# The ranking of edges by source runs inside the first walk, and part of its stores in the first node stage (graph network kernel, one core)

## The chip, the cores and the metric

The kernel runs on one core of a Trainium2 chip, as one program. The metric is the device time of that program in microseconds; the median of several runs is compared. The engines are TensorE (PE), VectorE (DVE), ScalarE (ACT), GpSimd (POOL) and SyncE (SP). Each has its own in-order queue of instructions and waits on semaphores. SP and ACT start ordinary transfers; indirect ones (gathers and scatters by an index per row) are started by GpSimd.

## The reference

Four layers of graph networks follow each other on 50000 nodes of 128 values and 25000 edges (src, dst), which come sorted by dst. The change touches the sort of the edges by source and the first layer alone:

```python
def _L0_gnn_ref(feat, W_neigh, b_neigh, src, dst):
    msgs = feat[src]
    neigh_sum = jax.ops.segment_sum(msgs, dst, num_segments=N)
    deg = jax.ops.segment_sum(jnp.ones(src.shape[0], feat.dtype), dst, num_segments=N)
    h_neigh = neigh_sum / jnp.maximum(deg, 1.0)[:, None]
    h = jnp.concatenate([feat, h_neigh], axis=1)
    return h @ W_neigh + b_neigh
...
def _gcn2_layer(x, W, beta, row, col, norm, num_nodes):
    h = jax.ops.segment_sum(norm[:, None] * x[col], row, num_segments=num_nodes)
    xp = (1.0 - ALPHA) * h + ALPHA * x
    return (1.0 - beta) * xp + beta * (xp @ W)
```

The result of each layer is added to its input and normalised. The second layer (two rounds of `_gcn2_layer`) sums over the edges of each source, so it needs the edges grouped by source. The layers behind it (two attention layers) use the order by dst.

## The kernel before

Nodes are padded and cut into 98 blocks of 512 rows and 196 tiles of 256 rows; edges into 196 columns of 128 edges (`J`), one edge per partition. The program is a row of phases; each ends with a barrier of all engines.

1. `lay_out_sorted` writes the edges in order of dst to memory and tests that they are sorted; they are, so two further sort passes are skipped.
2. `sort_pass` "s2" orders the edges by the upper digit of their source (196 digit values, 256 nodes each). VectorE makes one-hot rows of each column's digits, 28 groups of 7 columns (line 286), and TensorE sums them to a histogram (line 333). After prefix sums, the one-hots are made again; for each column TensorE adds the four columns before it to a running count (line 354), and VectorE reads each edge's place out of it (line 316, two instructions). VectorE writes the places of each group (line 321) and its payload, two words an edge, and GpSimd scatters them, one indirect store per column (line 365). Beside it, behind the ranks in the queues of TensorE and VectorE, the tables by dst are made: `walk_tables` "d" (lines 798 to 865) and `edge_tables` "e" (lines 471 to 521).
3. `walk_tables` "s" makes the same table by source ("sw_").
4. `walk` "e0" sums neighbours by dst. GpSimd gathers the source rows of the 196 columns (line 906); a table tells TensorE for each of 396 steps which column and which tile meet, each step being 2 products (4 matmuls in the trace, line 948) with one-hots of VectorE (line 921). ScalarE opens and empties the PSUM banks (lines 1018, 1021), SP stores each tile. A counter `ready` tells TensorE which gathers have landed.
5. `node_sage` goes over the 98 blocks in a pipeline of lags. Per block GpSimd does seven small instructions: the counts (`degree`, lines 1339 to 1343), the reciprocal root and shift (`deviation`, lines 1348 to 1352) and a factor (`factor`, line 1358). ScalarE's normalisation waits for the second, its store for the third. VectorE takes means and statistics (line 1451: the neighbour sums times the reciprocal degree), TensorE transposes and multiplies.
6. Two more walks by source, "e1a" and "e1b", and the other layers follow.

In the order listings below, and in the trace, a tile's name has its phase in front (`s_` or `e_`), and `e_bank` is the PSUM of the first walk.

Of the kernel before, what the change touches and what calls it, by code (L numbers as in the profile page):

```python
# [22 lines left out]
F32, I32, F16, BF16, U16 = mybir.dt.float32, mybir.dt.int32, mybir.dt.float16, mybir.dt.bfloat16, mybir.dt.uint16  # L23
ALU, ACT, AX = mybir.AluOpType, mybir.ActivationFunctionType, mybir.AxisListType

P = 128
# [4 lines left out]
SLOT = 6  # L31
NB = -(-NODES // BLOCK)
NPAD = NB * BLOCK
GC, SLOTS = 7, 4
TURN = GC * SLOTS
# [7 lines left out]
WS = 2  # L43
# [175 lines left out]

def sort_pass(nc, keep, name, words, digits, high, load, target, beside=None):  # L220

    with Phase(nc, name, freed="written") as ph:
# [26 lines left out]
        with nc.Block() as block:  # L251
            n_loads = load(block, ph, pay, loaded)
            more = ph.stack.enter_context(ExitStack())

# [104 lines left out]
            def _(pool):  # L359
# [8 lines left out]
                for s in range(SLOTS):  # L368
                    done(pool, scattered, TURNS - 1, s, 16 * GC)

            if beside is not None:
                with nc.allow_non_contiguous_dma(reason="one word of an edge's payload"):
                    beside(block, more, banks, lambda pe: pe.wait_ge(ranked, J + 4))

# [506 lines left out]

def walk(nc, keep, name, e, rows, table, summed, out, start):

# [4 lines left out]
    with Phase(nc, name) as ph:  # L888
# [7 lines left out]
        start.memory(ph)  # L896
        with nc.Block() as block:
            @block.gpsimd
            def _(pool):
                def landed(g):  # L900
                    pool.wait_ge(got[g % 7], 64 * (g // 7 + 1))
                    pool.sem_inc(ready, 1)

                for g in range(J // 4):
                    for c in range(4 * g, 4 * g + 4):
                        pool.indirect_dma_start(out=rows[:, c, 0:fetched], out_offset=None, in_=table,  # L906
                                                in_offset=bass.IndirectOffsetOnAxis(ap=e.other_i[:, c:c + 1], axis=0))\
                            .then_inc(got[g % 7], 16)
                    if g >= 2:
                        landed(g - 2)  # L910
                landed(J // 4 - 2)
                landed(J // 4 - 1)

            @block.vector
# [364 lines left out]

def node_sage(nc, keep, x_turned, agg, w, bias, y1):  # L1280

# [4 lines left out]
    with Phase(nc, "n0", freed="turned added stored y_ready x1_ready sums_ready meaned inverted") as ph:  # L1286
# [19 lines left out]
        sums_ready, rstd_ready, cleared, norm_step = (  # L1306
            slot_sems(ph, "sums_ready"), slot_sems(ph, "rstd_ready"), ph.sem("cleared"), ph.sem("norm_step"))
        with nc.Block() as block:
            @block.sync
# [19 lines left out]
            def _(pool):  # L1329
# [29 lines left out]

                pipeline(pool, (0, degree), (4, deviation), (4, factor))  # L1360

# [1585 lines left out]
def gnn(nc, x, x_turned, src, dst, attr, sage, gcn, gat2, gat, out):  # L2947
# [12 lines left out]
    with ExitStack() as stack:  # L2960
# [10 lines left out]
        with ExitStack() as walk_stack:  # L2971
            on_dst, lay_out_walk = walk_tables(nc, keep, "d", by_dst[1], WD, None, stack, krel_rows)

            def tables_on_dst(block, more, banks, banks_free):
                lay_out_walk(block, more, banks, banks_free)
                lay_out_edges(block, more, banks)

            sort_pass(nc, keep, "s2", WS, HIGH, True, load_edges(nc, src, dst, None), by_src, tables_on_dst)
            on_src = walk_tables(nc, keep, "s", by_src, WS, walk_stack)
            with nc.sbuf_tensor("x_rows", [P, J, ROW], F32) as rows:  # L2980
                walk(nc, keep, "e0", on_dst, rows, x, ROW, agg_dst, FromZero(ROW))
            node_sage(nc, keep, x_turned, agg_dst, sage["W"], sage["b"], y1)
            with nc.sbuf_tensor("y_rows", [P, J, ROW], F32) as rows:
                walk(nc, keep, "e1a", on_src, rows, y1, D, m1, FromRows(y1))
                walk(nc, keep, "e1b", on_src, rows, m1, D, z2, FromScaledRows(m1))
# [49 lines left out]
```

## Time and profile before

| | |
|---|---|
| median of 3 runs | 6525.23 us (6518.1 to 6535.32) |
| the profiled execution: its time | 6517.36 us |
| its span | 6515.6 us |
| TensorE busy | 3738.5 us, 57% |
| VectorE busy | 3242.0 us, 50% |
| ScalarE busy | 2301.1 us, 35% |
| GpSimd busy | 3518.2 us, 54% |
| mean granted clock of TensorE | 0.772 |

Busy shares are averages over stages with different limits, so no row of this table says what bounds one stage. Windows (stretches of the span in us from its start) and the timeline do. An indirect transfer counts on GpSimd as long as GpSimd makes its descriptors; its landing comes later.

### The profile page before, as it was taken

Reading aid. Unit: us, or ns where it says so; the run is one execution under the profiler, and the core shown is the slowest. Engines: PE = TensorE matmul, PEld = TensorE weight load, DVE = VectorE, ACT = ScalarE, POOL = GpSimd, SP = SyncE. Lnnn points to the kernel's source line nnn. Section 1 sums busy time; section 2 is a strip of 40 time slices with the busy share of each in tenths; the row PEclk is TensorE's granted clock in tenths of the full one; section 3 lists DMA queues with packets and bytes.
Section 4 is the critical chain, followed back from the end, with each engine's and each line's share of the span. In section 5 each row is a group of like instructions: output and inputs, shape, how many; then the busy total and the mean of one; then the engine's idle time right before and its main releaser. Section 6 shows DMA issues by size and latency. Waiting matters only on the chain. (4 is left out here: it accounts for less than half of the span.)

```text
span 6515.6 us, 102955 instructions
## 1 busy us (share of the span) xinstructions
PE 3738.5 (57%) x23719; PEld 2732.5 (42%) x23720; DVE 3242.0 (50%) x13277; ACT 2301.1 (35%) x6649; POOL 3518.2 (54%) x4631
## 2 busy tenths in 40 slices
PE   4421579715615685566669769998010089813566
PEld 3320568515615664233322256766010067612466
DVE  5330248503302485344467668886125178722577
ACT  0000347505504574233323258886000044400166
POOL 3647107771271055544406568887735755574398
PEclk7555799858857998888879889999555599955588
DMA  1012239625625796511101034443230189723276
GB/s 35 1 31 58 82 123 281 203 66 159 180 66 150 195 285 202 173 34 33 33 7 33 31 106 141 139 143 126 64 89 30 37 285 293 250 55 82 85 226 203
DMA packets 593072, 784.65 MB, mean 120 GB/s; under 512 B 138946, under 2 KB 362870, under 8 KB 592330
## 3 DMA queue, kind: packets, MB, share of 16 engines
q1 hardware_dynamic: 431734, 533.20, 27.0%
q0 software_dynamic: 62848, 112.43, 7.0%
q10 hardware_dynamic: 98328, 137.22, 5.7%
q8 instruction: 57, 0.93, 0.1%
q14 instruction: 105, 0.86, 0.0%
HBM read 470.23 MB, written 317.95 MB: 121 GB/s over the span
## 5 line engine op out<-in xcount | busy, mean ns | idle before, releaser
L2754 POOL TENSOR_SCALAR n_hot<-node_of,d_krel 128x256 f32<-128x256 f32 x396 | 366.6, 958 | 178.1 <-ACTq L2810 176.8
L1736 PE MATMUL lg_z_ps<-gat_wl,lg_tr 128*128 128x512 f32 x392 | 242.2, 703 | 254.1 <-issue 123.9
L948 PE MATMUL e_bank<-x_rows,e_hot 128*128 x1584 | 224.5, 292 | 273.1 <-issue 219.1
L948 PE MATMUL e1b_bank<-y_rows,e1b_hot 128*128 x1584 | 223.7, 290 | 270.4 <-issue 232.1
L948 PE MATMUL e1a_bank<-y_rows,e1a_hot 128*128 x1584 | 225.3, 291 | 265.3 <-issue 232.6
L1713 POOL DMA_INDIRECT lg_rows<-x,e_other_i x196 | 185.4, 946 | 311.2 <-PE lg_at_ps L1729 240.5
L906 POOL DMA_INDIRECT y_rows<-m,s_other_i x196 | 188.0, 959 | 306.4 <-POOLq L102 246.4
L1233 ACT ACTIVATE n_r<-n_r,n_shift,n_rstd 128x128 f32<-128x128 f32 x784 | 321.7, 480 | 79.0 <-POOL n_shift L1224 73.9
L689 POOL DMA_INDIRECT agg<-e_msg,e_put_i x196 | 193.7, 988 | 256.2 <-DVEq L718 195.8
L1792 DVE TENSOR_TENSOR lg_z<-lg_z_ps,lg_z 128x512 f32<-128x512 f32 x196 | 135.4, 691 | 391.4 <-issue 206.2
L948 PEld LDWEIGHTS e_bank<-x_rows,e_hot 128*128 128x128 f32 x1584 | 203.8, 201 | 294.1 <-issue 294.0
L948 PEld LDWEIGHTS e1b_bank<-y_rows,e1b_hot 128*128 128x128 f32 x1584 | 203.1, 202 | 291.1 <-issue 291.1
L948 PEld LDWEIGHTS e1a_bank<-y_rows,e1a_hot 128*128 128x128 f32 x1584 | 203.8, 203 | 287.1 <-issue 287.1
L2782 PE MATMUL n_bank<-h_rows,n_hot 128*128 x1584 | 248.0, 331 | 131.3 <-ACT n_bank L2816 113.3
L1499 POOL TENSOR_TENSOR n_rstd<-n_mv,minus_half 128x4 f32<-128x4 f32 x98 | 103.7, 1059 | 392.5 <-DVE n_mv L1592 392.5
L620 POOL DMA_INDIRECT agg_dst<-e_rows,e_put_i x196 | 203.3, 1037 | 194.6 <-DVEq L647 135.2
L921 DVE TENSOR_SCALAR e1b_hot<-node_of,s_krel 128x256 f32<-128x256 f32 x396 | 110.8, 350 | 386.1 <-remote 191.7
L921 DVE TENSOR_SCALAR e1a_hot<-node_of,s_krel 128x256 f32<-128x256 f32 x396 | 111.4, 352 | 379.0 <-issue 144.4
L921 DVE TENSOR_SCALAR e_hot<-node_of,d_krel 128x256 f32<-128x256 f32 x396 | 110.8, 350 | 378.5 <-remote 162.1
L2782 PEld LDWEIGHTS n_bank<-h_rows,n_hot 128*128 128x128 f32 x1584 | 240.4, 244 | 139.5 <-issue 139.5
L1233 ACT ACTIVATE n_o<-n_y_ps,n_shift,n_rstd 128x128 f32<-128x128 f32 x784 | 293.6, 458 | 13.0 <-POOL n_shift L1503 12.2
L365 POOL DMA_INDIRECT by_src<-s_pay_s,s_place_i x196 | 188.5, 962 | 171.9 <-DVE s_pay_s L322 112.8
(529 smaller groups left out, 12353.4 us busy)
## 6 DMA issues: line engine op xcount, KB each, us to landing
n_ag<-agg_dst SPq DMA_DIRECT2D x196, 264.0 KB, 3.8
n_hs<-h SPq DMA_DIRECT2D x196, 264.0 KB
n_xs<-x SPq DMA_DIRECT2D x196, 256.0 KB, 4.2
agg_dst<-e_ev SPq DMA_DIRECT2D x196, 132.0 KB
y<-n_o ACTq DMA_DIRECT2D x98, 264.0 KB, 3.5
e1a_fed<-y SPq DMA_DIRECT2D x196, 132.0 KB
m<-e1a_ev SPq DMA_DIRECT2D x196, 132.0 KB
e1b_fed<-m SPq DMA_DIRECT2D x196, 132.0 KB
```

Source lines behind the costliest of these rows:

```text
L365: pool.indirect_dma_start(out=target, out_offset=bass.IndirectOffsetOnAxis(ap=place_i[:, s, k:k + 1], axis=0), in_=pay_s[:, s, k, :], in_o ...
L620: pool.indirect_dma_start(out=agg, out_offset=bass.IndirectOffsetOnAxis(ap=e.put_i[:, c:c + 1], axis=0), in_=rows[:, c, :], in_offset=None ...
L689: pool.indirect_dma_start(out=agg, out_offset=bass.IndirectOffsetOnAxis(ap=e.put_i[:, c:c + 1], axis=0), in_=msg[:, g % SLOTS, k, 0:out_wi ...
L906: pool.indirect_dma_start(out=rows[:, c, 0:fetched], out_offset=None, in_=table, in_offset=bass.IndirectOffsetOnAxis(ap=e.other_i[:, c:c + ...
L921: ins = dve.tensor_scalar(hot[:, s, k, :], keep.node_of[:, :], e.krel[:, bass.ds(turn * (HOTS * STEPB) + s * STEPB + k, 1)], None, ALU.is_ ...
L948: ins = pe.matmul(bank[:, bass.ds(to + h * width, summed)], hot[:, s, k, h * P:(h + 1) * P], flat_rows[:, bass.ds(row, summed)], start=Fal ...
L1233: ins = act.activation(out[:, g, 0:D], r[:, g, :], ACT.Identity, bias=shift[:, g:g + 1], scale=rstd[:, g:g + 1])
L1713: pool.indirect_dma_start(out=rows[:, g % SLOTS, k, i, :], out_offset=None, in_=x, in_offset=bass.IndirectOffsetOnAxis(ap=of[:, c:c + 1], ...
L1736: pe.matmul(z_ps[q][:, :], tr[:, q, 0, :], g.wl[:, :], start=True, stop=False)
L1792: dve.tensor_tensor(z[:, c % 2, :], z_ps[c % 2][:, :], z[:, c % 2, :], ALU.max).then_inc(z_out, 1)
L2754: ins = pool.tensor_scalar(hot[:, i // STEPB % HOTS, i % STEPB, :], keep.node_of[:, :], e.krel[:, i:i + 1], None, ALU.is_equal)
L2782: ins = pe.matmul(bank[:, bass.ds(to + h * 256, SUMMED)], hot[:, s, k, h * P:(h + 1) * P], flat_rows[:, bass.ds(row, SUMMED)], start=False ...
```

## The change

The sort by source is no phase of its own. The tables by dst are made in a phase "t" without it. A class `BySource` makes the ranks at the head of the first walk's instructions on VectorE and TensorE (`rank`), using the walk's PSUM. GpSimd first starts the walk's 196 gathers, then scatters the first `EARLY` = 112 columns (`scatter_early`). The 84 others are scattered in `node_sage`, one per block, by a fourth stage `sort` of GpSimd's pipeline, which is now written out instead of a loop. Places and payload of all columns stay in memory on the chip. The table by source comes after `node_sage`.

```diff
+EARLY = 112
...
+class BySource:
...
+    def rank(self, nc, keep, ph, block, banks):
...
+        @block.scalar
+        def _(act):
+            act.wait_ge(ends_in, 16 * WS)
+            for i in range(WS):
+                act.activation(pay[:, :, i], ends[:, i, :], ACT.Copy).then_inc(loaded, 1)
...
+            with dve.Fori(0, TURNS) as turn:
+                for s in range(SLOTS):
+                    dve.wait_ge(hot_used, turn * SLOTS + s + 1)
+                    hot(turn, s, digs_ready, first_hot)
...
+                    for k in range(GC):
+                        c = s * GC + k
+                        dve.wait_ge(run_ready, turn * TURN + c + 1)
+                        dve.tensor_tensor_reduce(junk[:, c % 4, :], onehot[:, s, k, :], run_ps[c % 4][:, 0:digits],
+                                                 1.0, 0.0, ALU.mult, ALU.add, place[:, s, k:k + 1]).then_inc(ranked, 1)
+                    dve.wait_ge(ranked, turn * TURN + (s + 1) * GC + 4)
+                    dve.tensor_copy(self.place_i[:, bass.ds(turn * TURN + s * GC, GC)], place[:, s, :]).then_inc(self.placed, 1)
...
+            pe.wait_ge(ranked, J + 4)
...
+    def scatter_early(self, pool):
+
+        pool.wait_ge(self.loaded, WS)
+        for c in range(EARLY):
+            pool.wait_ge(self.placed, c // GC + 1)
+            self.scatter(pool, c, self.scattered[c // 4 % 7])
+            if c % 4 == 3 and c >= 11:
+                g = c // 4 - 2
+                pool.wait_ge(self.scattered[g % 7], 64 * (g // 7 + 1))
+        for g in (EARLY // 4 - 2, EARLY // 4 - 1):
+            pool.wait_ge(self.scattered[g % 7], 64 * (g // 7 + 1))
+        pool.wait_ge(self.placed, J // GC)
...
         with nc.Block() as block:
+            if by_source is not None:
+                by_source.rank(nc, keep, ph, block, bank[:, :].rearrange("p (b w) -> p b w", b=RING))
+
...
                 landed(J // 4 - 2)
                 landed(J // 4 - 1)
+                if by_source is not None:
+                    by_source.scatter_early(pool)
...
-                pipeline(pool, (0, degree), (4, deviation), (4, factor))
+                def sort(turn, s):
+
+                    k = turn * SLOT + s
+                    c = k + EARLY
+                    if k >= 8 and c - 8 < J:
+                        pool.wait_ge(sorted_in[k % 8], 16 * (k // 8))
+                    if c < J:
+                        by_source.scatter(pool, c, sorted_in[k % 8])
+
+                pipeline(pool, (0, degree), (4, deviation), (4, factor), (0, sort), written_out=True)
...
-            sort_pass(nc, keep, "s2", WS, HIGH, True, load_edges(nc, src, dst, None), by_src, tables_on_dst)
...
+            with ExitStack() as source_stack:
+                by_source = BySource(nc, source_stack, src, dst, by_src)
+                with nc.sbuf_tensor("x_rows", [P, J, ROW], F32) as rows:
+                    walk(nc, keep, "e0", on_dst, rows, x, ROW, agg_dst, FromZero(ROW), by_source)
+                node_sage(nc, keep, x_turned, agg_dst, sage["W"], sage["b"], y1, by_source)
             on_src = walk_tables(nc, keep, "s", by_src, WS, walk_stack)
-            with nc.sbuf_tensor("x_rows", [P, J, ROW], F32) as rows:
-                walk(nc, keep, "e0", on_dst, rows, x, ROW, agg_dst, FromZero(ROW))
-            node_sage(nc, keep, x_turned, agg_dst, sage["W"], sage["b"], y1)
```

Three places where the order of instructions moves. TensorE at the head of the first walk, before: the banks are opened by 8 matmuls and the loop of the walk begins.

```order
L928 MATMUL e_bank<-iota_h,ident_h 128x264 x8
L932 UNCONDITIONAL_BRANCH
L932 ISA
L937 TENSOR_LOAD d_table
L937 ISA
```

TensorE at the same place of the changed kernel (its own line numbers): histogram loop, sums, then the loop of the ranks (its first rows).

```order
L971 MATMUL e_bank<-iota_h,e_zero_h 128x196
L973 UNCONDITIONAL_BRANCH
L973 ISA
L977 MATMUL e_bank<-e_onehot,ident_h 128x196 x7
...
L980 MATMUL e_bank<-iota_h,e_zero_h 128x196
L983 MATMUL e_bank<-e_hist,ones_h 128x196
L984 MATMUL e_bank<-e_hist,tri_h 128x196
L987 MATMUL e_bank<-e_base,ident 128x196 x4
L989 UNCONDITIONAL_BRANCH
L989 ISA
L996 MATMUL e_bank<-e_onehot,ident_h 128x196 x4
```

The rows of before come after these loops now. GpSimd in the walk and up to the first block of the node stage, changed kernel; before, line 906 (now 1048) was followed by the barrier at once:

```order
L1048 DMA x_rows<-x,d_other_i 128x128 x196
L1004 DMA by_src<-by_src_pay,by_src_place_i 25088x2 x112
L1036 UNCONDITIONAL_BRANCH
L101 ISA
L1473 UNCONDITIONAL_BRANCH
L1484 TENSOR_TENSOR n_q<-n_ag,ones 128x4
L1486 TENSOR_TENSOR n_part<-n_q,n_ninths 128x4
L1488 TENSOR_TENSOR n_part<-n_part,ones 128x4
```

112 stores stand between the last gather and the end of the phase. GpSimd in the loop of the node stage before, from one block's counts to the next one's:

```order
L1339 TENSOR_TENSOR n_q<-n_ag,ones 128x4
L1341 TENSOR_TENSOR n_part<-n_q,n_ninths 128x4
L1169 REGISTER_ALU
L1343 TENSOR_TENSOR n_part<-n_part,ones 128x4
L1348 TENSOR_TENSOR n_rstd<-n_mv,minus_half 128x4
L1169 ISA
L1350 TENSOR_TENSOR n_shift<-n_mv,n_rstd 128x4
L1169 REGISTER_ALU
L1352 TENSOR_TENSOR n_shift<-n_shift,minus_one 128x4
L1358 TENSOR_TENSOR n_o<-n_part,n_q 128x4
```

And in the changed kernel:

```order
L1484 TENSOR_TENSOR n_q<-n_ag,ones 128x4
L1486 TENSOR_TENSOR n_part<-n_q,n_ninths 128x4
L1488 TENSOR_TENSOR n_part<-n_part,ones 128x4
L1493 TENSOR_TENSOR n_rstd<-n_mv,minus_half 128x4
L1495 TENSOR_TENSOR n_shift<-n_mv,n_rstd 128x4
L1497 TENSOR_TENSOR n_shift<-n_shift,minus_one 128x4
L1503 TENSOR_TENSOR n_o<-n_part,n_q 128x4
L1004 DMA by_src<-by_src_pay,by_src_place_i 25088x2
```

The register instructions are gone, and one store stands between a block's factor and the next block's counts.

## Rows read from the trace of the kernel before

**Rows 1.** Windows of scatters, of the walk with gathers and without, of the node stage.
```profile
86.00:258.00 172.00, 73.50 (x440) 55.96 (x440) 66.53 (x372) 0.00 (x0) 107.75 (x112) 0.56 0.02 1
...
455.00:690.00 235.00, 31.59 (x86) 23.44 (x86) 7.13 (x24) 6.76 (x20) 176.98 (x185) 0.51 0.22 57
...
712.00:940.00 228.00, 181.50 (x1445) 169.78 (x1444) 98.20 (x354) 122.61 (x364) 0.00 (x0) 0.98 0.31 109
957.00:1238.00 281.00, 272.72 (x2037) 229.08 (x2038) 232.11 (x1156) 208.08 (x667) 207.17 (x673) 0.99 0.87 274
```

**Rows 2.** Tile x_rows: matmuls and gathers, ns min/median/max, first and last start.
```profile
L948 PE MATMUL e_bank<-x_rows,e_hot x1584: 276/276/585, 447.0 to 938.8; 128*128 x198
L906 POOL DMA_INDIRECT x_rows<-x,d_other_i x196: 940/944/1795, 440.3 to 687.7; - x196
```

**Rows 3.** Timeline of TensorE in the first walk: start us, us, instruction, idle before.
```profile
439.54 1.92 PE L928 MATMUL e_bank<-iota_h,ident_h 128*128 128x264 f16 x8 [4.15 <-PEq L102]
446.98 8.01 PE L948 MATMUL e_bank<-x_rows,e_hot 128*128 x44 [5.52 <-POOLq L902]
...
501.94 0.38 PE L948 MATMUL e_bank<-x_rows,e_hot 128*128 x1 [2.41 <-issue]
...
712.63 0.38 PE L948 MATMUL e_bank<-x_rows,e_hot 128*128 x1 [1.03 <-issue]
714.76 1.23 PE L948 MATMUL e_bank<-x_rows,e_hot 128*128 x4 [1.75 <-issue]
```

**Rows 4.** Windows: attention edges with and without gathers, attention sum, first and later part.
```profile
2800.00:3200.00 400.00, 274.80 (x839) 133.82 (x840) 183.68 (x1024) 127.82 (x419) 194.54 (x205) 0.82 0.13 34
3300.00:3345.00 45.00, 44.69 (x158) 22.40 (x157) 32.42 (x185) 23.51 (x78) 0.00 (x0) 1.00 0.00 0
4935.00:4980.00 45.00, 0.00 (x0) 0.00 (x0) 40.58 (x91) 0.00 (x0) 34.35 (x34) 0.50 0.12 40
4980.00:5080.00 100.00, 0.00 (x0) 0.00 (x0) 33.17 (x76) 0.00 (x0) 77.45 (x75) 0.50 0.12 39
```

**Rows 5.** Timeline of GpSimd and VectorE around the table work.
```profile
32.73 0.36 POOL L394 CAST s_pay<-s_ends 128x196 f32<-128x196 int32 x1 [19.49 <-DMA s_ends<-dst]
...
384.49 0.40 DVE L798 CAST dw_key_i<-dw_pay 98x256 int32<-98x256 f32 x1
...
422.73 0.15 DVE L516 TENSOR_SCALAR e_split<-et_whole 128x1 f32<-128x1 f32 x1
...
438.08 0.57 DVE L836 SCALAR_TENSOR_TENSOR s_krel<-sw_tile_off,sw_banks 128x396 f32<-128x396 f32 x1
```

**Rows 6.** The sort: line 333, then timeline of VectorE and GpSimd.
```profile
L333 PE MATMUL s_banks<-s_onehot,ident_h x196: 245/257/373, 36.4 to 76.5; 128*128 128x196 f16 x196
...
85.23 0.17 DVE L321 CAST s_place_i<-s_place 128x7 int32<-128x7 f32 x1
...
91.45 0.17 DVE L321 CAST s_place_i<-s_place 128x7 int32<-128x7 f32 x1
...
86.44 1.22 POOL L365 DMA_INDIRECT by_src<-s_pay_s,s_place_i  x1 [53.05 <-DVE s_pay_s L322]
...
262.86 1.01 POOL L365 DMA_INDIRECT by_src<-s_pay_s,s_place_i  x1 [4.73 <-DVE s_pay_s L322]
```

**Rows 7.** Timeline of GpSimd and VectorE in the node stage.
```profile
956.82 0.73 POOL L1343 TENSOR_TENSOR n_part<-n_part,ones 128x4 f32<-128x4 f32 x1
...
956.79 0.69 DVE L1451 TENSOR_TENSOR n_ag<-n_ag,n_rq 128x512 f32<-128x512 f32 x1
...
1100.56 1.01 POOL L1348 TENSOR_TENSOR n_rstd<-n_mv,minus_half 128x4 f32<-128x4 f32 x1 [0.39 <-DVE n_mv L1440]
...
1102.77 0.20 POOL L1343 TENSOR_TENSOR n_part<-n_part,ones 128x4 f32<-128x4 f32 x1
1103.40 1.01 POOL L1348 TENSOR_TENSOR n_rstd<-n_mv,minus_half 128x4 f32<-128x4 f32 x1 [0.43 <-DVE n_mv L1440]
```

**Rows 8.** Line 620: indirect stores beside VectorE work, ns min/median/max.
```profile
L620 POOL DMA_INDIRECT agg_dst<-e_rows,e_put_i x196: 977/982/1887, 4935.6 to 5197.3; - x196
```

More of the change, by code:

```diff
@@ L217, in _, with sort_pass @@
                 dve.tensor_copy(keep.ident_b[:, :], keep.ident[:, :])
-def sort_pass(nc, keep, name, words, digits, high, load, target, beside=None):
+def sort_pass(nc, keep, name, words, digits, high, load, target):
     with Phase(nc, name, freed="written") as ph:
@@ L252, in sort_pass @@
             n_loads = load(block, ph, pay, loaded)
-            more = ph.stack.enter_context(ExitStack())
             @block.sync
@@ L369, in _ @@
                     done(pool, scattered, TURNS - 1, s, 16 * GC)
-            if beside is not None:
-                with nc.allow_non_contiguous_dma(reason="one word of an edge's payload"):
-                    beside(block, more, banks, lambda pe: pe.wait_ge(ranked, J + 4))
 def load_edges(nc, src, dst, attr):
@@ L887, in walk @@
+def walk(nc, keep, name, e, rows, table, summed, out, start, by_source=None):
     width, fetched = out.shape[1], table.shape[1]
@@ L1277, in pipeline, with node_sage @@
         steps(turn, True)
-def node_sage(nc, keep, x_turned, agg, w, bias, y1):
+def node_sage(nc, keep, x_turned, agg, w, bias, y1, by_source):
     with Phase(nc, "n0", freed="turned added stored y_ready x1_ready sums_ready meaned inverted") as ph:
@@ L1307, in node_sage @@
             slot_sems(ph, "sums_ready"), slot_sems(ph, "rstd_ready"), ph.sem("cleared"), ph.sem("norm_step"))
+        sorted_in = [ph.sem(f"sorted_in{n}") for n in range(8)]
         with nc.Block() as block:
@@ L2972, in gnn @@
             on_dst, lay_out_walk = walk_tables(nc, keep, "d", by_dst[1], WD, None, stack, krel_rows)
-            def tables_on_dst(block, more, banks, banks_free):
-                lay_out_walk(block, more, banks, banks_free)
-                lay_out_edges(block, more, banks)
-            sort_pass(nc, keep, "s2", WS, HIGH, True, load_edges(nc, src, dst, None), by_src, tables_on_dst)
+            with Phase(nc, "t") as ph, ExitStack() as more, nc.allow_non_contiguous_dma(reason="one word of an edge's payload"):
+                banks = ph.ps("banks", [P, 8, 512])
+                with nc.Block() as block:
+                    lay_out_walk(block, more, banks, lambda pe: None)
+                    lay_out_edges(block, more, banks)
+            with ExitStack() as source_stack:
[3 more added lines that the diff above has]
+                node_sage(nc, keep, x_turned, agg_dst, sage["W"], sage["b"], y1, by_source)
             on_src = walk_tables(nc, keep, "s", by_src, WS, walk_stack)
-            with nc.sbuf_tensor("x_rows", [P, J, ROW], F32) as rows:
-                walk(nc, keep, "e0", on_dst, rows, x, ROW, agg_dst, FromZero(ROW))
-            node_sage(nc, keep, x_turned, agg_dst, sage["W"], sage["b"], y1)
             with nc.sbuf_tensor("y_rows", [P, J, ROW], F32) as rows:
```

92 lines of the change are left out of this document (91 added, 1 removed).

## The prediction

> **What bounds the kernel now.** One core, one program in a row of stages; only the stages up to the end of the first node stage are touched, so I read these as a chain of stages. The windows by stage come first [rows 1]. In each window the busy time and count of TensorE, its weight loads, VectorE, ScalarE and GpSimd stand in that order, then the granted clock. GpSimd streams 112 scatters in 172 us, then 185 gathers in 235 us. While it gathers, TensorE does 86 matmuls in 235 us; when it has stopped, 1445 in 228 us.
>
> The timeline of TensorE shows what happens [rows 3]. The walk starts at 447.0 with 44 matmuls in 8 us; soon after, single matmuls stand alone with 2.4 us of "issue" before them, a mean of 235 / 86 = 2.73 us each. The pace returns at 714.8, some 26 us after the last gather (it starts at 687.7 [rows 2]). Nothing in the rows names a data wait. The same happens to VectorE in the attention sum, where GpSimd stores without a break: 91 instructions in the first 45 us, then 76 in 100 us [rows 4]. So a long stream of indirect transfers slows the issue of the other engines, after a first stretch that goes at full pace. In the sort the same two engines make the ranks while GpSimd scatters; GpSimd runs out of places after every 14 scatters, and the others catch up then.
>
> In the node stage TensorE is the bound: 272.7 of 281 us busy, granted clock 0.99, so the upper level of 2.4 GHz [rows 1]. 98 blocks take 281 us, 2.87 us each. GpSimd's chain for one block goes from 1100.56 to 1102.97, 2.41 us; then it waits 0.43 us for VectorE [rows 7].
>
> **The change, term by term: the front.** All times from the span's start; "before" the walk's last matmul starts at 938.8 [rows 2].
> 1. The tables alone. Their source is there at about 33 (the loads land then [rows 5]). The work itself stays as it was: 384.49 to 422.88, 38.4 us. The next stage begins 1.6 us after the last table instruction (438.65 to the first gather at 440.3). The first gather is at 73.
> 2. 196 gathers: 440.3 to 687.7, and 1 more, 248.4 us: until 321.5. The slow pace lasts another 26 us: 347.5.
> 3. What of the ranking gets done beneath them? It starts with a histogram, 28 groups of 7 matmuls, all fed by one-hots of VectorE. At full pace it takes 36.4 to 76.7, so 1.44 us a group [rows 6]. Matmuls that have to be issued in the shadow cost 2.73 us, so 19 us a group. Some 6 groups pass before the pace falls (it fell 15 us after the first gather), then 347.5 - 73 - 15 = 259 us give 13 or 14. 8 are left: 11.5 us, 359. Even if this count is off by 5 groups it is 7 us; the shadow of the gathers is worth little in either direction.
> 4. From the last histogram matmul (76.7) to the first scatter (86.4): 9.7 us, 369.
> 5. 112 scatters with the ranks made beside them, as in the sort: from the 1st at 86.44 to the 113th at 262.86, 176.4 us [rows 6]: 545. The 11 groups of ranks that are still missing then have GpSimd quiet, at 6.22 us each (85.23 to 91.45 [rows 6]): 68.4 us, 613.5.
> 6. Only now can TensorE and VectorE begin the walk, since its instructions stand behind the ranks in their queues. Start 7.4 us (439.54 to 446.98 [rows 3]). Then all 396 steps of 4 matmuls at full pace: 1445 matmuls in the 224 us from 714.8 to 938.8 are 0.62 us a step, 245.5 us. The walk ends at 866.5.
> So the front is 938.8 - 866.5 = 72 us shorter. The sort's own time is not hidden; what is saved is the slow scattering of the last 84 columns, and the gathers' dead time, of which the histogram uses a piece. The walk table by source is only moved behind the node stage; it fills most of the 16 us from 422.9 to 438.7 [rows 5] and is in the sum of neither side as a change.
>
> **The node stage.** 84 scatters are added to GpSimd's queue, one per block. Each takes 247.4 / 195 = 1.27 us of it [rows 2]. GpSimd becomes the bound: 2.41 + 1.27 = 3.68 us. VectorE's 0.69 us instruction of line 1451 comes once per block, and beside it a GpSimd instruction of 0.20 us took 0.73 [rows 7]; a scatter covers a third of the block, so I add 0.2 us as an estimate: 3.88. That is 1.01 us more than 2.87, for 84 blocks 85 us. Behind the scatter in the same queue stand the counts of the next block, then the reciprocal root that ScalarE waits for; TensorE waits for ScalarE to free its bank, so the whole chain takes GpSimd's pace. Bounds: 3.61 us (no lengthening, register instructions gone because the loop is written out), 62 us; above, every scatter as slow as the worst of the attention sum, 1.89 instead of 0.98 us [rows 8], so 4.6 us, 145 us.
> Do the other engines starve here too? In the attention-edge stage GpSimd is 49% busy, and VectorE does 1024 / 400 = 2.56 instructions per us beside it, 185 / 45 = 4.11 without [rows 4]: a loss of 38%. Here the scatters are a quarter of the time; in proportion that is 19%, 2.87 / 0.81 = 3.55 us. It stays below GpSimd's 3.88. The clock should stay up: with TensorE 80% busy it was 0.98 [rows 1].
>
> The Trainium skill, "SBUF — State Buffer", section "SBUF: two separate sides", says that GpSimd cannot write the descriptors of its transfers while VectorE holds the shared port pair, and that a transfer of 620 ns then took some 3100. The trace agrees that such a lengthening exists (0.20 to 0.73 us [rows 7]), but not with that size. By the page's figures the 84 scatters would cost 208 us more, a time near 6750.
>
> **Sum.** -72 + 85 = +13 us. The profiled execution took 6517.4 us, so 6530; the median of the runs is 7.9 above it, 6525.2, so 6538. A measurement of this kernel tells 0.3%, 20 us, from no change; I expect nothing that can be told.
>
> **Rivals.**
> Forecast: front 60 to 85 shorter, node stage 75 to 95 longer: 6515 to 6560. Chance 0.46.
> Scatters in the node stage cost more (ends slower). Place: GpSimd's queue in the first node stage. With +0.53 us from VectorE's port in nearly every one, and some waiting for them, a block takes 4.4 us: +129 - 72 = +57, 6582; at 4.6 us, 6598. It decides above 2.87 + 92 / 84 = 3.97 us a block. For it: the median of line 620 hides a maximum of twice that. Against: VectorE's long two-input instruction is only a quarter of a block. Chance 0.25.
> The node stage takes them lightly. The written-out loop has fewer instructions and the wait of 0.43 us vanishes; if a block takes 3.4 us: +45 - 72 = -27, 6498. Against: 2.41 us of dependent instructions can't shrink much. Chance 0.17.
> The ranking does get done beneath the gathers. If the histogram and three rank groups pass there, 11.5 and 3 times 11 us go: 6493, chance 0.09. If nothing is slowed there: histogram, bridge and 28 x 6.2 are 224 us, less than 248; the 112 scatters then stand alone (142 us) and the walk ends near 712: 6383, chance 0.03. For it: the sort's loops ran well beside its own scatters. Against: there GpSimd paused after every 14, and the gathers start every 1.27 us to the end [rows 2].
> The Trainium skill, "Runtime: NRT & Kernel Launch", section "Instruction fetch mechanics", says that fetching instructions is mostly hidden behind their dispatch. By that rule alone this last case would be the likely one; the trace, with 2.73 us between matmuls that wait for nothing, speaks against it, though it does not say what starves.
>
> **Numbers.** Faster: 0.12 of the ranking cases, 0.11 of the light one, 0.03 of the forecast's edge: 0.26. Slower: 0.25 and 0.11 of the forecast's edge: 0.36. Same: 0.38. The range takes front 50 to 95 and node stage 62 to 145: 6485 to 6610, leaving out the extreme cases.
>
> **What the profile would show.** Right: the first gather near 73; in the gathers' shadow some 20 groups of histogram matmuls, one per 2.7 us; first scatter near 370; walk from 621 to 867; in the node stage a scatter of about 1 us after each block, GpSimd without idle time, TensorE 75% busy, blocks of 3.9 us. Wrong: ranks made during the gathers; blocks well above or below 3.9; scatters on the early side that wait for their landing; a walk whose steps are slower than 0.62 us.

## The result, and the profile after

The changed kernel takes 6590 us (median of four runs, 6574.5 to 6600.7) against 6524 (6518.1 to 6535.3) before: 1.0098 times as long, 95% interval 1.0073 to 1.0122. It is slower by 0.7 to 1.2%. The profiled execution took 6574.5 us, its span is 6572.8, 57 us more than before.

The windows of the trace after, by stage, in the columns of [rows 1]: the gathers, the scatters with the ranks, the ranks alone, the walk, the node stage.

```profile
85.00:300.00 215.00, 17.23 (x91) 11.52 (x91) 19.46 (x96) 0.00 (x0) 162.86 (x172) 1.00 0.20 52
363.00:545.00 182.00, 82.78 (x498) 63.00 (x497) 72.34 (x399) 0.00 (x0) 109.01 (x112) 0.57 0.02 1
545.00:598.00 53.00, 34.02 (x289) 29.66 (x286) 42.06 (x233) 0.00 (x0) 0.00 (x0) 0.82 0.00 0
602.00:847.00 245.00, 197.75 (x1583) 185.78 (x1584) 107.84 (x389) 132.92 (x393) 0.00 (x0) 0.99 0.32 108
875.00:1279.00 404.00, 311.37 (x2028) 264.21 (x2026) 226.86 (x1156) 219.79 (x676) 333.55 (x748) 0.88 0.57 185
```

Tiles and lines of the same trace (ns min/median/max, first and last start): histogram matmuls, gathers, the cast of each group's places, scatters, the walk's matmuls, and the reciprocal root, once a block, which marks the node stage's ends; last an addition of the factor, of which more below.

```profile
L977 PE MATMUL e_bank<-e_onehot,ident_h x196: 245/369/373, 76.7 to 357.3; 128*128 128x196 f16 x196
L1048 POOL DMA_INDIRECT x_rows<-x,d_other_i x196: 942/947/1795, 71.5 to 319.1; - x196
L966 DVE CAST by_src_place_i<-e_place x28: 170/171/226, 367.4 to 598.6; 128x7 f32 x28
L1004 POOL DMA_INDIRECT by_src<-by_src_pay,by_src_place_i x196: 967/972/1052, 368.3 to 1228.8; - x196
L1092 PE MATMUL e_bank<-x_rows,e_hot x1584: 276/276/579, 602.1 to 847.0; 128*128 x198
L1493 POOL TENSOR_TENSOR n_rstd<-n_mv,minus_half x98: 1001/1042/1050, 875.2 to 1278.7; 128x4 f32<-128x4 f32 x98
L1488 POOL TENSOR_TENSOR n_part<-n_part,ones x98: 199/720/725, 864.9 to 1267.2; 128x4 f32<-128x4 f32 x98
```

The lines of the root and of that addition in the kernel before:

```profile
L1348 POOL TENSOR_TENSOR n_rstd<-n_mv,minus_half x98: 1006/1006/1049, 966.7 to 1242.9; 128x4 f32<-128x4 f32 x98
L1343 POOL TENSOR_TENSOR n_part<-n_part,ones x98: 198/199/726, 956.8 to 1231.4; 128x4 f32<-128x4 f32 x98
```

Windows of after with the tile of the places alone (VectorE's casts, then GpSimd's scatters): 16 groups have their places when the 112th scatter is done, 12 come behind it.

```profile
360.00:537.00 177.00, 2.81 (x16) 109.01 (x112) 0.57 0.02 1
537.00:599.00 62.00, 2.05 (x12) 0.00 (x0) 0.78 0.00 0
```

The stage's last root and the next walk's first gather, in the timeline of before and in that of after:

```profile
1242.88 1.01 POOL L1348 TENSOR_TENSOR n_rstd<-n_mv,minus_half 128x4 f32<-128x4 f32 x1 [0.78 <-DVE n_mv L1440]
1250.52 1.02 POOL L906 DMA_INDIRECT y_rows<-y,s_other_i  x1 [5.92 <-POOLq L102]
```

```profile
1278.71 1.01 POOL L1493 TENSOR_TENSOR n_rstd<-n_mv,minus_half 128x4 f32<-128x4 f32 x1 [0.81 <-DVE n_mv L1594]
1303.57 1.03 POOL L1048 DMA_INDIRECT y_rows<-y,s_other_i  x1 [23.15 <-POOLq L102]
```

These rows close the account. The walk's last matmul starts at 847.0 instead of 938.8: -91.8. The node stage lasts 403.5 instead of 276.2 us: +127.3. From its last root to the next gather it is 24.9 instead of 7.6 us: +17.2, the walk table by source, which now stands there alone. With 0.3 us at the node stage's start that is +53.0, the whole shift of that gather (1250.5 to 1303.6). The other 4 us of the 57 come later.

One block of the node stage on GpSimd, from the timeline of after, and VectorE beside it:

```profile
1002.10 1.03 POOL L1004 DMA_INDIRECT by_src<-by_src_pay,by_src_place_i  x1 [0.38 <-issue]
1003.16 0.21 POOL L1484 TENSOR_TENSOR n_q<-n_ag,ones 128x4 f32<-128x4 f32 x1
1003.46 0.20 POOL L1486 TENSOR_TENSOR n_part<-n_q,n_ninths 128x4 f32<-128x4 f32 x1
1003.73 0.72 POOL L1488 TENSOR_TENSOR n_part<-n_part,ones 128x4 f32<-128x4 f32 x1
1004.41 1.04 POOL L1493 TENSOR_TENSOR n_rstd<-n_mv,minus_half 128x4 f32<-128x4 f32 x1
...
1005.96 0.20 POOL L1503 TENSOR_TENSOR n_o<-n_part,n_q 128x4 f32<-128x4 f32 x1
1006.54 1.04 POOL L1004 DMA_INDIRECT by_src<-by_src_pay,by_src_place_i  x1 [0.38 <-issue]
1007.62 0.21 POOL L1484 TENSOR_TENSOR n_q<-n_ag,ones 128x4 f32<-128x4 f32 x1
```

```profile
1003.47 0.20 DVE L1603 RECIPROCAL n_rq<-n_q 128x8 f32<-128x8 f32 x1 [1.88 <-POOL n_q L1484]
1003.70 0.69 DVE L1605 TENSOR_TENSOR n_ag<-n_ag,n_rq 128x512 f32<-128x512 f32 x1
```

GpSimd waits for no other engine, and a block takes it 1007.62 - 1003.16 = 4.46 us. Everyone else waits for it: VectorE 1.88 us for the counts, and that wait locks the two engines in step. VectorE's long two-input instruction (line 1605) now starts 0.54 us after the counts in every block, just when GpSimd makes the addition of line 1488, and that takes 0.72 us instead of 0.20. Before, VectorE had its own pace, and the two met only now and then [rows 7]: the addition's median was 199 ns, its maximum 726; now the median is 720.

The histogram beneath the gathers looks other than I had forecast. In the first window it has 91 matmuls in 215 us, one per 2.4 us on average, which is 16.5 us for a group of seven. But they don't come one by one. TensorE's timeline between two groups:

```profile
313.56 1.33 PE L977 MATMUL e_bank<-e_onehot,ident_h 128*128 128x196 f16 x7 [18.23 <-issue]
331.76 1.33 PE L977 MATMUL e_bank<-e_onehot,ident_h 128*128 128x196 f16 x7 [16.87 <-DVE e_onehot L937]
```

Seven matmuls go in 1.33 us, then TensorE stands for 17 to 18 us, in the second row until VectorE's one-hots are there. VectorE, which does 96 instructions in these 215 us, is the one that comes late here.

### The profile page after: what moved, and what is told of

It is laid out like the page before. It is cut to its first block and busy times, and to the rows that moved or that the text cites. A ratio compares the mean times of both kernels' runs of the same rounds, so it can differ in the third digit from the quotient of the medians.

```text
span 6572.8 us, 102475 instructions
## 1 busy us (share of the span) xinstructions
PE 3746.1 (57%) x23719; PEld 2742.4 (42%) x23720; DVE 3245.9 (49%) x13248; ACT 2318.4 (35%) x6651; POOL 3590.6 (55%) x4629
## 5 line engine op out<-in xcount | busy, mean ns | idle before, releaser
L2908 POOL TENSOR_SCALAR n_hot<-node_of,d_krel 128x256 f32<-128x256 f32 x396 | 382.3, 979 | 179.5 <-ACTq L2964 177.8
L1867 POOL DMA_INDIRECT lg_rows<-x,e_other_i x196 | 186.8, 953 | 298.3 <-PE lg_at_ps L1883 228.0
L1004 POOL DMA_INDIRECT by_src<-by_src_pay,by_src_place_i x196 | 195.7, 999 | 138.8 <-DVE by_src_place_i L966 76.1
L1258 PE MATMUL e_xl_ps<-gat_wl,e_xg 128*128 128x512 f32 x392 | 241.2, 700 | 43.8 <-DVEq L1287 19.1
L1162 ACT ACTIVATE e_bank<-e_zeros 128x264 f32<-128x264 f32 x203 | 78.9, 391 | 525.8 <-PE e_bank L1072 525.8
L1048 POOL DMA_INDIRECT x_rows<-x,d_other_i x196 | 189.1, 965 | 117.6 <-POOLq L102 58.1
```

The lines of the kernel that those rows point to most:

```text
L1004: return pool.indirect_dma_start(out=self.target, out_offset=bass.IndirectOffsetOnAxis(ap=self.place_i[:, c:c + 1], axis=0), in_=self.pay[ ...
L1258: pe.matmul(self.xl_ps[k][:, :], xg[:, s % 2, k, :], self.wl[:, :], start=True, stop=False)
L1867: pool.indirect_dma_start(out=rows[:, g % SLOTS, k, i, :], out_offset=None, in_=x, in_offset=bass.IndirectOffsetOnAxis(ap=of[:, c:c + 1], ...
L2908: ins = pool.tensor_scalar(hot[:, i // STEPB % HOTS, i % STEPB, :], keep.node_of[:, :], e.krel[:, i:i + 1], None, ALU.is_equal)
```

## The experiments

The ratios are to runs of the kernel before on the same chip, whose medians lay between 6520 and 6538 us.

**1. All scatters in the front.**

```
-EARLY = 112
+EARLY = 196
```

> All 196 scatters by source stand behind the gathers in the front; the node stage has none, everything else is the changed kernel. Theory 1 (GpSimd's queue is what the scatters lengthen in the node stage): the node stage goes back from 404 to 276 us, -127. The front grows by 84 scatters: the 112 took 168.6 us from 368.3 on, 1.505 us each, so 196 take 295 and end near 663 instead of the last ranks at 599: +64. Sum 6590 - 63 = 6527, between 6510 and 6545. Theory 2 (the written-out loop or the tables kept in the stage cost the 127 us): the node stage stays near 400 us, 6650.

Measured: 6523.9 us, 0.9987 of before (0.9978 to 0.9997).

```profile
L1493 POOL TENSOR_TENSOR n_rstd<-n_mv,minus_half x98: 1006/1007/1050, 942.7 to 1220.8; 128x4 f32<-128x4 f32 x98
L966 DVE CAST by_src_place_i<-e_place x28: 170/171/291, 366.5 to 660.9; 128x7 f32 x28
```

The node stage is back at 278 us, with the tables kept and the loop written out: the scatters make all of its 127 us. The last places come at 660.9, 62 us later than with 112 scatters, so a scatter more, beside the ranks, costs 62 / 84 = 0.74 us here, against 127 / 84 = 1.5 in the node stage. Theory 2 is dead.

**2. The written-out loop alone**, in the kernel before: `pipeline(pool, ..., (4, factor), written_out=True)`, no scatter.

> The kernel before, with GpSimd's program of the first node stage written out instead of looped, and no scatter in it. Theory 1: no change, 6524 within 10 us, 2.87 us a block. Theory 2 (the written-out program itself slows GpSimd or the engines beside it): up to 1.6 us a block, 98 blocks, 6680; half of that would be 6600.

Measured: 6523.3 us, 0.9992 (0.9982 to 1.0003); no price, as expected.

**3. The scatter elsewhere in GpSimd's block.** Right behind the counts:

```
                     pool.tensor_tensor(q[:, s, 0, :], ag[:, s, :, D], keep.ones[:, 0:GB], ALU.add).then_inc(counted[s], 1)
+                    sort(turn, s)
...
-                pipeline(pool, (0, degree), (4, deviation), (4, factor), (0, sort), written_out=True)
+                pipeline(pool, (0, degree), (4, deviation), (4, factor), written_out=True)
```

> The same 84 scatters, but each right behind the first GpSimd operation of a block (the counts plus one), ahead of the two that make the factor. VectorE's 0.69 us two-input instruction, which begins 0.54 us after that operation, now lies beneath the scatter and no longer beside the GpSimd addition that took 0.72 instead of 0.20 us. Theory 1 (the elementwise GpSimd instruction is lengthened by VectorE's, the scatter is not): a block takes 4.46 - 0.52 = 3.94 us, 44 us less over 84 blocks: 6546. Theory 3 (what VectorE holds up is GpSimd itself, a scatter as well): the scatter takes 0.5 us or more longer, a block 4.4 to 4.6 us, 6585 to 6610.

Measured: 6579.4 us, 1.0082 (1.0067 to 1.0097). From its timeline of GpSimd:

```profile
1004.12 0.20 POOL L1492 TENSOR_TENSOR n_q<-n_ag,ones 128x4 f32<-128x4 f32 x1
1004.74 1.51 POOL L1004 DMA_INDIRECT by_src<-by_src_pay,by_src_place_i  x1 [0.42 <-issue]
...
1006.57 0.20 POOL L1497 TENSOR_TENSOR n_part<-n_part,ones 128x4 f32<-128x4 f32 x1
```

Theory 1 fell, theory 3 holds in its mechanism: the addition is back at 0.20 us, but the scatter, now beneath VectorE's instruction, takes 1.51 instead of 1.04. The 0.5 us has moved with the place. A block takes 4.31 us, a little less than theory 3's 4.4 to 4.6, and the time lies 6 us below its range.

**4. The reciprocal root behind the counts**, all else as in the changed kernel:

```
-                pipeline(pool, (0, degree), (4, deviation), (4, factor), (0, sort), written_out=True)
+                pipeline(pool, (0, count), (4, deviation), (0, degree), (4, factor), (0, sort), written_out=True)
```

> The changed kernel with the same GpSimd instructions and the same scatters in the node stage, in another order: right behind the counts comes the reciprocal root, then the two operations of the factor, its product, and the scatter. VectorE's 0.69 us instruction still begins 0.54 us after the counts, now beneath the reciprocal root (which in the kernel before took 1.01 us beside it, no longer than alone). Theory 3a (VectorE's instruction holds up the access of GpSimd's, and the root, one long computation, hardly notices): nothing is lengthened by 0.5 us, a block takes 4.46 - 0.52 = 3.94 us, 6546. Theory 3b (VectorE's instruction takes 0.5 us from GpSimd whatever lies beside it): a block stays at 4.3 to 4.46 us, 6575 to 6595.

Measured: 6525.0 us, 1.0002 (0.9988 to 1.0016).

```profile
1001.35 0.21 POOL L1482 TENSOR_TENSOR n_q<-n_ag,ones 128x4 f32<-128x4 f32 x1
1001.50 1.04 POOL L1494 TENSOR_TENSOR n_rstd<-n_mv,minus_half 128x4 f32<-128x4 f32 x1
...
1005.12 0.21 POOL L1482 TENSOR_TENSOR n_q<-n_ag,ones 128x4 f32<-128x4 f32 x1
```

```profile
1001.88 0.69 DVE L1606 TENSOR_TENSOR n_ag<-n_ag,n_rq 128x512 f32<-128x512 f32 x1
```

Theory 3a holds and more: a block takes 3.77 us, 0.69 less. VectorE's instruction of 0.69 us, from 1001.88 on, lies inside the root, and neither is longer than elsewhere in these traces. That is the 0.52 us. Most of the rest is at the counts: the multiplication behind them waited for their end and began 0.30 us after their start, the root needs nothing of them and begins after 0.15. The same instructions in another order undo the loss of the change, so its time is that of the kernel before: the node stage still takes 349 us instead of 276, and the front pays for it.

**5. Less on GpSimd**: the factor's two operations and its product go to VectorE.

```
-                    st(pool.tensor_tensor(part[:, s, :], q[:, s, 0, :], ninths[:, :], ALU.mult))
-                    st.wait()
-                    pool.tensor_tensor(part[:, s, :], part[:, s, :], keep.ones[:, 0:GB], ALU.add).then_inc(mixed[s], 1)
...
-                    pool.tensor_tensor(o[:, s, :, D + 1], part[:, s, :], q[:, s, 0, :], ALU.mult).then_inc(added[s], 1)
...
+                    dve.tensor_scalar(part[:, s, :], q[:, s, 0, :], 2.0 / 9.0, 1.0, ALU.mult, ALU.add).then_inc(mixed[s], 1)
...
+                    dve.tensor_tensor(o[:, s, :, D + 1], part[:, s, :], q[:, s, 0, :], ALU.mult).then_inc(added[s], 1)
```

> The changed kernel, with the two operations that make the factor and their product moved from GpSimd to VectorE; GpSimd keeps the counts, the reciprocal root, the shift and the scatter. Theory 1 (GpSimd's queue is the bound): its chain for a block is 0.20 + 1.12 + 0.28 + 0.59 + 1.06 = 3.25 us instead of 4.46 (starts to starts in the steady part), VectorE has about 3.0; a block takes 3.3 us, 84 x 1.16 = 97 us less, 6493. Theory 4 (the issue of the other engines starves beside the scatters whatever GpSimd's own load is): at the 38% loss of the attention-edge stage a block takes 4.0 to 4.4 us, 6550 to 6585.

Measured: 6471.6 us, 0.9911 (0.9895 to 0.9926), faster than before.

Its window of 200 us in the node stage, and the counts of two blocks in its timeline:

```profile
900.00:1100.00 200.00, 187.04 (x1411) 157.07 (x1410) 165.96 (x940) 149.42 (x471) 176.52 (x336) 1.00 0.88 270
```

```profile
1001.65 0.21 POOL L1483 TENSOR_TENSOR n_q<-n_ag,ones 128x4 f32<-128x4 f32 x1
1004.63 0.21 POOL L1483 TENSOR_TENSOR n_q<-n_ag,ones 128x4 f32<-128x4 f32 x1
```

A block takes 2.98 us with a scatter in it. TensorE does 1411 matmuls in 200 us, 7.1 per us against 7.25 in [rows 1], at the granted clock of 1.00, though GpSimd is 88% busy. So theory 4 is dead: nobody starves beside one scatter per block.

**6. Transfers spread over the front.** That left a puzzle: 86 matmuls in 235 us beside a stream of gathers [rows 1], next to no loss beside one scatter in 3 us. So the gathers get waits, and the 112 early scatters go into the walk:

```
+    def pace(self, pool, c):
+        if c < J // GC:
+            pool.wait_ge(self.first_hot, c + 1)
+        elif (c - J // GC) % (GC - 1) == 0:
+            g = (c - J // GC) // (GC - 1)
+            pool.wait_ge(self.placed if g else self.base_ready, g or 1)
...
+            pool.wait_ge(steps_done, (HOTS + c // 2) * STEPB)
             self.scatter(pool, c, self.scattered[c // 4 % 7])
```

> The changed kernel with its transfers spread in the front: one gather behind each of the 28 one-hot groups of the histogram, six behind each of the 28 groups of ranks; the first 112 scatters stand in the walk, two at each batch of six steps. The node stage is that of the changed kernel. Theory 5 (a transfer costs the other engines 0.68 us as long as GpSimd pauses in between; this is what the 84 scatters cost that are in the front of one kernel and not of the other, (660.9 - 603)/84): histogram 28 x (1.44 + 0.68) = 59, bridge 10, ranks 28 x (6.0 + 6 x 0.68) = 282, last ranks near 423; walk 245 + 112 x 0.68 = 321, ends near 750 instead of 847; 6590 - 97 = 6493. Theory 6 (the others get nothing done beside a transfer, spread or not): histogram 75, ranks 28 x 13.6 = 381, walk 387, ends near 925: 6668.

> The same spreading, with 98 scatters in the walk and 98 in the node stage, whose factor VectorE makes as in the earlier run (2.97 us a block). Theory 5: walk 245 + 98 x 0.68 = 312, ends near 739, 113 us earlier than in that run; 14 blocks more with a scatter add 2 us: 6472 - 111 = 6361. Theory 6: walk ends near 905 instead of 852: 6525 to 6550.

Measured: 6360.7 us, 0.9752 (0.9740 to 0.9765); with 98 scatters in the walk and the factor on VectorE 6245.4, 0.9569 (0.9557 to 0.9581). Both expectations were far too modest. The window of paced_front over its walk, then its row of places:

```profile
388.00:631.00 243.00, 197.17 (x1582) 185.21 (x1583) 116.35 (x391) 131.56 (x394) 115.27 (x112) 0.99 0.33 110
```

```profile
L966 DVE CAST by_src_place_i<-e_place x28: 170/171/425, 129.3 to 383.8; 128x7 f32 x28
```

The histogram of paced_and_vector, in its timeline of GpSimd: one gather a group.

```profile
99.25 0.94 POOL L1058 DMA_INDIRECT x_rows<-x,d_other_i  x1 [0.53 <-issue]
100.72 0.94 POOL L1058 DMA_INDIRECT x_rows<-x,d_other_i  x1 [0.53 <-issue]
```

With 112 scatters beside it the walk takes 243 us, as with none. In the histogram, where the release by VectorE's one-hots leaves 0.53 instead of 0.30 us between two gathers, a group takes 1.47 us, against 1.44 alone and 16.5 beneath the unbroken gathers of the changed kernel. Only where six gathers come in one go, beside the ranks, is there a price: (383.8 - 129.3) / 27 = 9.4 us a group, against 5.1 for the ranks alone (the twelve groups in 62 us above).

**7. One wait undone.** The kernel of paced_front without the line `pool.wait_ge(steps_done, ...)`: the same scatters in the same walk, back to back.

> The kernel of paced_front with one thing undone: the 112 scatters stand in the walk as there, but GpSimd doesn't wait for the walk's batches between them and issues them back to back from the start of the walk. Theory 7 (it is the unbroken stream that starves the others; with a pause, be it 0.2 us more between two transfers, they lose nothing: in paced_front the walk with 112 scatters took 242.7 us, as without any): the stream lasts 112 x 1.27 = 142 us; 15 us at full pace, some 127 us and 10 us after it at 2.7 us a matmul, so 50 matmuls instead of 880; the walk takes about 375 instead of 243 us, 6361 + 130 = 6490. Theory 8 (scatters of 8 bytes a row cost the walk nothing, paced or not, as they touch neither its rows nor its queues): 6361.

Measured: 6502.9 us, 0.9971 (0.9956 to 0.9986), 142 us more than paced_front. The same 133 us of the walk, first here, then in paced_front:

```profile
403.00:536.00 133.00, 18.34 (x51) 13.84 (x51) 3.82 (x12) 4.16 (x13) 99.45 (x103) 0.50 0.04 8
```

```profile
403.00:536.00 133.00, 106.18 (x863) 99.51 (x863) 65.14 (x216) 73.52 (x220) 74.49 (x73) 1.00 0.34 111
```

51 matmuls against 863, with 103 scatters against 73. The whole walk takes 384 us (its matmuls start from 389.4 to 773.2) instead of 243, near the 375 of theory 7. GpSimd is three quarters busy in one window and more than half in the other; it is the unbroken stream that starves TensorE, and the engines that work with it stand too. Theory 8 is dead. The wait changes two things at once, the rests and the number of transfers in a given time. The histogram of experiment 6 speaks for the rests: there a gather started every 1.47 us, which is 90 in 133 us, and cost nothing.

**8. How fine must the spreading be?** Gathers released one by one by the ranks (`pool.wait_ge(self.ranked, 4 + GC * g + k)`), six to a group; then four to a group, the other 56 in the walk, two at a batch, with the scatters behind them.

> The kernel of paced_and_vector, with the six gathers of a rank group released one after each of its ranks and no longer six at once. Theory 7: a group is bounded below by its own 5.6 to 6.2 us and by GpSimd's six transfers, 7.6 us; it takes 7.6 to 8.2 us instead of 9.4, 28 groups save 34 to 50 us: 6195 to 6211. Theory 9 (only GpSimd's busy share counts, not how the transfers are spread): a group stays at 9.4 us, 6245 within 10.

> The kernel of paced_and_vector, with four instead of six gathers to a group of ranks, each behind another rank; the other 56 gathers stand in the walk, two at a batch of six steps, ahead of the 98 scatters, which follow in the last 38 batches. Theory 7: four transfers are 5.1 us, less than a group's own 6 us, so with pauses the ranks run at their own pace: 28 x 6.0 = 168 us, last ranks near 300 instead of 385, and the walk still takes 243 us, with two to three transfers to 3.7 us: ends near 546, 6245 - 87 = 6158. Theory 9 (busy share: 0.57 us for each gather beside the ranks): 28 x 8.1 = 227, 6209; and the walk, with GpSimd 80% busy instead of 50%, takes 20 to 50 us longer: 6230 to 6260.

Measured: 6231.5 us, 0.9562 (0.9545 to 0.9579), and 6189.6, 0.9492 (0.9477 to 0.9507). Timeline of GpSimd in one_by_one, then the rows of places of one_by_one and of gathers_shared:

```profile
251.56 0.95 POOL L1060 DMA_INDIRECT x_rows<-x,d_other_i  x1 [3.13 <-DVE e_place L963]
252.82 0.95 POOL L1060 DMA_INDIRECT x_rows<-x,d_other_i  x1 [0.30 <-issue]
```

```profile
L966 DVE CAST by_src_place_i<-e_place x28: 170/171/183, 127.0 to 374.6; 128x7 f32 x28
```

```profile
L966 DVE CAST by_src_place_i<-e_place x28: 170/171/393, 128.1 to 298.3; 128x7 f32 x28
```

The first missed: 9.2 us a group, not 7.6 to 8.2. Ranks left alone come faster (5.1 us for seven) than GpSimd can start six gathers (7.5), so it falls behind its releases and the stream is unbroken again, until the ranks starve and it has to wait 3.13 us for one. With four to a group it keeps up: (298.3 - 128.1) / 27 = 6.3 us. That is near my 6.0, but not free: it is 1.2 us more than the ranks alone, 0.3 us for each gather. TensorE was granted 0.69 in this stage and 0.82 in the window of the ranks alone, so part of it can be the clock; no run separates the two. The walk with 154 transfers took 260 instead of 243 us, 17 of the 32 us by which this stayed above its expectation. Another 8 us lie between the walk's last matmul and the node stage's first root (36 us instead of the 28 of paced_and_vector); the rest was not traced.

**9. Nothing but a pause**, in the three walks of the kernel before:

```
                             .then_inc(got[g % 7], 16)
+                        pool.memset(idle[:, :], 0.0).then_inc(tick, 1)
+                        pool.wait_ge(tick, c + 1)
```

> The kernel before with one thing added in its three walks: behind each gather GpSimd clears four words of a spare tile and waits for that to be done, so that two gathers are some 0.3 us further apart. No order of work is changed, no wait on another engine is added. In the paced histogram 0.23 us more between gathers left the matmuls their full pace. Theory 7a (a short pause of GpSimd is enough, whatever makes it): the gathers of a walk take 196 x 1.55 = 304 us and the walk runs beneath them, so about 320 us instead of 492 to 498, three walks save 3 x 175 = 525: 6000. Theory 7b (what helped the others was that GpSimd stood at a wait for another engine, or the longer rests in between; 0.3 us of its own does nothing): the gathers take 304 instead of 247 us with the others still starved, 3 x 57 = 171 us more: 6695.

Measured: 6287.3 us, 0.9620 (0.9604 to 0.9636). Windows of the first walk, while gathers run and after:

```profile
455.00:732.00 277.00, 194.78 (x841) 165.99 (x842) 59.86 (x198) 68.43 (x204) 199.86 (x369) 0.64 0.30 93
732.00:846.00 114.00, 93.45 (x743) 87.87 (x744) 50.09 (x180) 62.98 (x188) 1.09 (x2) 0.98 0.32 114
```

Between the two theories: 841 matmuls beneath the gathers instead of 86, half of the walk and not all of it. Tile x_rows of this run:

```profile
L951 PE MATMUL e_bank<-x_rows,e_hot x1584: 272/276/585, 455.7 to 846.0; 128*128 x198
L907 POOL DMA_INDIRECT x_rows<-x,d_other_i x196: 943/952/2092, 439.1 to 732.0; - x196
```

From its first matmul to its last the first walk takes 390 us instead of 492 [rows 2], the two later ones 399 and 401 instead of 482 and 486. From gather to gather it is 1.34 us three times and 1.9 the fourth time, where GpSimd waits for the landing of an older group of four and counts it; over the walk it is 293 / 195 = 1.50 us. In the timeline of the plain stream it is 1.25 us also there. So the clear gives two kinds of rest, 0.09 us at each gather and some 0.6 us more at every fourth, and this run doesn't tell which of them helps.

**10. Two clears, and all that helped.** The kernel of gathers_shared, with two such clears behind each gather of the two later walks.

> The kernel of gathers_shared, and in its two later walks two short clears of GpSimd behind each gather instead of the one of pause_each. There one clear (1.34 us from gather to gather instead of 1.27) brought a walk from 492 to 390 us; two should be 1.7 us apart, so the gathers take 337 us. Theory 7 (the longer the rest between two transfers, the less the others starve): the walk keeps up and ends some 15 us behind the last gather, 350 us; two walks save 2 x 142 = 284: 6190 - 284 = 5906. Theory 7c (half of the starvation stays with any pause of this size): a walk takes 390 us or, with the slower gathers, up to 430: 5990 to 6065.

Measured: 5913.8 us, 0.9054 (0.9036 to 0.9072). Tile y_rows, the first of the two walks:

```profile
L1111 PE MATMUL e1a_bank<-y_rows,e1a_hot x1584: 274/275/577, 944.2 to 1276.9; 128*128 x198
L1063 POOL DMA_INDIRECT y_rows<-y,s_other_i x196: 952/952/1080, 925.3 to 1257.2; - x196
```

The gathers are 1.70 us apart on average (mostly 1.50, every fourth time some 2.1) and last 332 us instead of 247, and the walk ends 20 us behind them, 352 us after the first one, as expected; before it was 492 (1250.5 to 1742.1). The transfers are slower, and the stage is 140 us shorter.

## Why the prediction was right and wrong

The time, 6590, lay in the range, but the likeliest case did not come: I gave "no change" 0.38 and forecast 6538. What came is the first rival, the scatters costing more in the node stage (4.4 us a block, 6582, chance 0.25). That even the rival's time was nearly hit is partly luck: it put the front's gain 20 us too low and left out the 17 us of the table by source, and the two nearly cancel. By the steps of the prediction:

- **Steps 1 to 4** held to 2 us: gathers from 71.5 to 319.1, the last eight histogram groups after the pace came back, first scatter at 368.3. The number of histogram groups in the shadow was right, 20. Their form was not: the matmuls came seven at once behind VectorE's late one-hots, and not one per 2.7 us.
- **Step 5** was too long by 15 us: the 112 scatters took 169 us instead of 176, and the twelve groups left over 5.1 us each (61.6), where I had put eleven at 6.22, a pace that I had read beside scatters.
- **Step 6**: the start took 3.5 instead of 7.4 us; the walk's 245 us were right. The front gave 92 us, not 72.
- **The sum**: an error of bookkeeping. The 16 us of the table by source were left out of the new front and counted in the old one, so they were in the 72 us as saved; I wrote that they were in neither side. They come back behind the node stage as 17.2 us.
- **The node stage**: the mechanism was right (GpSimd becomes the bound, all wait for it, the others don't starve). The size was not. I added 1.27 + 0.20 us to GpSimd's chain of 2.41; measured are 4.46 - 2.41 = 2.05: about 1.5 for the scatter, since from the start of the product to that of the next counts it is 1.66 us instead of 0.15, and 0.52 for VectorE's hold. The 0.2 us was an average over chance meetings. Once GpSimd is the bound, VectorE waits for the counts and its instruction meets the same GpSimd instruction in every block. Experiments 3 and 4 show both the hold and that it hangs on the order; 1 and 2 exclude the written-out loop and the kept tables.

So -72 + 85 = +13 became -92 + 127 + 17 = +52, and 4 us later on.

I had expected the clock to stay up. TensorE was granted 0.88 on average in the node stage, between the levels of 1.2 and 2.4 GHz; from 900 to 1270 us it waits up to 1.8 us for ScalarE in 55 of some 88 blocks, 72 us in all. ScalarE waits for GpSimd, so TensorE has time to spare and the clock should cost nothing; no run tests that alone. In experiment 5, where these waits are short, the clock is 1.00 again.

On the hold, the Trainium skill, "SBUF — State Buffer", section "SBUF: two separate sides", says that a VectorE instruction with two inputs in SBUF and a GpSimd one that reads it exclude each other for the whole instruction. The rows agree that a 0.20 us addition and a scatter are held up (by 0.52 and 0.47 us). The factor of five that the prediction quoted is the section's figure beside a copy on VectorE and not beside an instruction with two inputs; here the scatter took half as long again. The rows don't agree on the whole instruction: VectorE's 0.69 us ran inside the root's 1.04 us, and neither was lengthened.

No case of mine held what the experiments found beyond the change. I had noted that the sort's loops ran well beside their scatters, and that GpSimd paused there after every 14, but took it as a reason against a rival and not as a thing that can be made.

Open is what it is that runs dry on the other engines. The rows say only "issue": no data, no semaphore. The Trainium skill, "Runtime: NRT & Kernel Launch", section "Instruction fetch mechanics", calls the fetch mostly hidden; no run here shows whether it is the fetch that starves. The queue that brings instructions moved 1 packet in the 133 us of walk_stream and 3 in those of paced_front, which doesn't settle it. Nor was it tried how short a rest may be, or whether other instructions of GpSimd than these clears make one.

## What to carry to other kernels

In this kernel a stream of indirect transfers on GpSimd without a break all but stopped the engines beside it (51 matmuls against 863). With rests, by a wait on the consumer or by idle clears, the same transfers cost the histogram and the walk of 112 scatters nothing, the ranks 0.3 us each. How much an idle clear gives depends on its length: one brought a walk from 492 to 390 us, two to 352. Look for single instructions with some 2.4 us of "issue" before them, and try to pace the stream. When an engine becomes the bound, others can fall into step with it: here a conflict that had hit now and then hit in every block, and the order of the instructions could place it where it cost nothing. And what a change moves must be booked on both sides.

## What the runs showed of the hardware

- Matmuls of the walk beside a stream of transfers 1.25 to 1.27 us apart: one per 2.6 to 2.7 us (51 in 133 us in walk_stream, 86 in 235 us before). With one clear between them, 1.50 us on average: 841 in 277 us. With an even 1.47 us (histogram), and with two scatters per 3.7 us (walk of paced_front): full pace.
- VectorE starves too: 96 instructions in 215 us beneath the gathers of the changed kernel.
- An indirect scatter beside a two-input VectorE instruction of 0.69 us took 1.51 instead of 1.04 us (scatter_behind_q), an addition 0.72 instead of 0.20 (the changed kernel); a reciprocal root of 1.04 us was not lengthened (root_behind_q).
